# Sigmoid-weighted pooling on one core: goods loads issued at four places of an iteration, left-over weights laid out one copy at a time

## The chip, the cores and the metric

The kernel runs on one core of a Trainium2 chip. The metric is the device time in microseconds of one execution. Before the change the median of three runs is 299.17 us (297.19 to 300.1).

## The reference, cut to what matters

For each of B = 2048 rows there are N = 200 goods vectors of K = 32 numbers and one candidate vector of 32. The outer product of candidate and goods, the goods and the candidate go through a 1088 x 36 layer, a sigmoid and a 36 x 1 layer; the scalar weight that comes out weighs the goods, which are summed over N:

```python
outer = jnp.einsum('bi,bnj->bnij', candidate_ad, goods).reshape(Bs, Ns, Ks * Ks)
k_b = jnp.broadcast_to(candidate_ad[:, None, :], (Bs, Ns, Ks))
h1 = jnp.concatenate((k_b, goods, outer), axis=-1)
act = jax.nn.sigmoid(h1 @ W1 + b1)
weight = act @ W2 + b2
out = jnp.sum(goods * weight, axis=1)
```

All data are float32. goods is 52.4 MB and is read once.

## The kernel before

The outer product is never formed. In a setup stage the kernel folds each candidate into the first layer, so that each row has its own 32 x 36 weight (`wm` for the first 32 outputs, `wx` for the left-over 4). After that goods is streamed once.

Four rows are a unit, 8 units are a "pair" (two halves `s` of four units), and 64 pairs (`PAIRS`) are worked through in a software pipeline with `LAG` = 3. In iteration p of the main loop TensorE does, in this order:

1. `products(p)` (L267): 64 matmul records, goods times `wm`, into `z_ps` (or `s_ps`);
2. `spread(p - 3, 0)` (L332): spreads the weights of an older pair over partitions;
3. `row_sums(p - 1)` (L309): the second layer of the pair before, 24 records;
4. `products_x(p)` (L286): the left-over 4 outputs, 16 records;
5. `spread(p - 3, 1)` (L332).

ScalarE applies the sigmoids: eight `act` activations (L378; `act_done` counts up after each second one) and then one `actx` (L383, `actx_done`). VectorE takes the weights out of PSUM (`whole`, L408, `w_kept`) and pools pair p - 3 (L416; `pooled` counts up four times per pair, twice behind each `spread`). GpSimd splits the weights into three bf16 parts (L206, L208, L210, L215).

**Goods loads.** A pair is 800 KB, loaded by four DMAs of 200 KB, all issued by SyncE (SP) at L173. There are seven slots (`G_SLOTS`). The first seven pairs are loaded without a wait. From then on load j of pair p waits only for its own quarter of the slot: `pooled >= 4 * (p - 7) + j + 1`. So a load starts when VectorE has pooled that quarter of pair p - 7; `POOLED_ORDER` puts the quarters in the order in which they come free.

**Left-over weights.** `wx` is needed in a padded layout, which GpSimd writes in 8 chunks of 8 pairs. `lay_out(k)` (L189) makes the four copies of a chunk (L194). Two chunks are laid out before the loop; chunks 2 to 7 in the loop, all four copies in a row behind the split of every eighth pair. `products_x` waits at L277 for the chunk at each eighth pair.

**Instruction queue.** Each engine's program reaches it in 16 KB packets over the same DMA engines that carry goods; in the profile they are the packets of kind "instruction".

Of the kernel before, what the change touches and what calls it, by code (L numbers as in the profile page):

```python
# [13 lines left out]
HX = H - HM  # L14
UNITS = B // 4
PAIR_U = 8
PAIRS = UNITS // PAIR_U
G_SLOTS = 7
A_SLOTS = 3
LAG = 3  # L20
T_MAIN = HM // 4
# [2 lines left out]
WX_CHUNK = 8  # L24
# [18 lines left out]
def build(nc, goods_t, cand_r, cand_u, w1_outer, small, pick, out_t):  # L43
    with ExitStack() as ctx:
        def sb(name, shape, dt=F32):
            return ctx.enter_context(nc.sbuf_tensor(name, shape, dt))
# [4 lines left out]
        def sem(name):  # L51
            return ctx.enter_context(nc.semaphore(name))

        goods = sb("goods", [P, G_SLOTS, PAIR_U, N])
        wm = sb("wm", [P, UNITS // RUN, HM, RUN])
        wxd = sb("wxd", [P, UNITS // 2, 2, HX])
        warm = sb("warm", [P, 1])
        wx = sb("wx", [P, UNITS // 2, 3, 16])
        act = sb("act", [P, A_SLOTS, 4, 2 * N])
        actx = sb("actx", [P, A_SLOTS, N])  # L60
        consts = sb("consts", [P, C_ALL])
# [67 lines left out]
        pick_loaded = sem("pick_loaded")  # L129
        goods_loaded = [sem(f"goods_loaded{i}") for i in range(G_SLOTS)]  # L130
        out_stored = sem("out_stored")
        warm_set = sem("warm_set")
        wx_step = sem("wx_step")
# [4 lines left out]
        z_done = sem("z_done")  # L138
        x_done = sem("x_done")
        act_done = sem("act_done")  # L140
        actx_done = sem("actx_done")
# [8 lines left out]
        def kept(i, x):  # L150

            return 2 * i + x // 2 + 1
# [7 lines left out]
        @block.sync  # L160
        def _(sp):
            sp.dma_start(cand[:, :, :], cand_r[:, :, :]).then_inc(cand_loaded, 16)
            sp.dma_start(candu[:, :], cand_u[:, :]).then_inc(candu_loaded, 16)

            sp.wait_ge(w1_loaded, 16)
            sp.wait_ge(consts_loaded, 16)
            for p in range(PAIRS):
                for j, v in enumerate(POOLED_ORDER):
                    if p >= G_SLOTS:

                        sp.wait_ge(pooled, 4 * (p - G_SLOTS) + j + 1)
                    first = N * (PAIR_U * p + v)
                    sp.dma_start(goods[:, p % G_SLOTS, v:v + 2, :].rearrange("p u n -> p (u n)"),  # L173
                                 goods_t[:, first:first + 2 * N]).then_inc(goods_loaded[p % G_SLOTS], 16)
                q = p - G_SLOTS
                if q >= 0 and q % STORE == STORE - 1:
                    first = PAIR_U * (q + 1 - STORE)
                    sp.dma_start(out_t[:, first:first + PAIR_U * STORE],
                                 out_stage[:, first:first + PAIR_U * STORE]).then_inc(out_stored, 16)
            sp.wait_ge(pooled, 4 * PAIRS)  # L180
            first = PAIR_U * (PAIRS - STORE)
            sp.dma_start(out_t[:, first:], out_stage[:, first:]).then_inc(out_stored, 16)
            sp.wait_ge(out_stored, 16 * (PAIRS // STORE))

        @block.gpsimd
        def _(pool):
            nc.gpsimd.memset(wx[:, :, :, :], 0.0).then_inc(wx_step, 1)

            def lay_out(k):  # L189

                of = slice(4 * WX_CHUNK * k, 4 * WX_CHUNK * (k + 1))
                for r in range(4):
                    rows = slice(32 * r, 32 * r + 32)
                    nc.gpsimd.tensor_copy(wx[rows, of, 0::2, HX * r:HX * r + HX], wxd[rows, of, :, :]).then_inc(wx_step, 1)  # L194
                    pool.wait_ge(wx_step, 4 * k + r + 2)

            pool.wait_ge(wx_step, 1)

            pool.wait_ge(wb_kept[0], kept(0, 2))
            pool.wait_ge(wb_kept[1], kept(0, 3))  # L200
            for k in range(WX_AHEAD):
                lay_out(k)
            pool.wait_ge(consts_loaded, 16)
            for q in range(PAIRS):
                pool.wait_ge(w_kept, q + 1)
                nc.gpsimd.tensor_scalar(top[:, :], whole[:, q % 2, :], m1, None, ALU.mult).then_inc(part_step, 1)  # L206
                pool.wait_ge(part_step, 4 * q + 1)
                nc.gpsimd.tensor_tensor(rest[:, :], whole[:, q % 2, :], top[:, :], ALU.subtract).then_inc(part_step, 1)  # L208
                pool.wait_ge(part_step, 4 * q + 2)
                nc.gpsimd.tensor_scalar(mid[:, :], rest[:, :], m2, None, ALU.mult).then_inc(part_step, 1)  # L210
                pool.wait_ge(part_step, 4 * q + 3)
                if q >= 2:

                    pool.wait_ge(s_done, 2 * (q - 1))
                nc.gpsimd.tensor_tensor(stack[:, q % 2, :], rest[:, :], mid[:, :], ALU.subtract).then_inc(part_step, 1)  # L215
                k = q // WX_CHUNK + WX_AHEAD
                if q % WX_CHUNK == 0 and k < PAIRS // WX_CHUNK:
                    pool.wait_ge(part_step, 4 * q + 4)
                    lay_out(k)

        @block.tensor
        def _(pe):
# [68 lines left out]
            def row_sums(p, step):  # L291
# [10 lines left out]
                for t in range(4):  # L302

                    if step < 2:
                        first = N * (t // 2)
                        left, right = w2m[:, step, :], act[:, p % A_SLOTS, 2 * (t % 2) + step, first:first + N]
                    else:
                        left, right = w2x[:, t, :], actx[:, p % A_SLOTS, :]
                    last = nc.tensor.matmul(w_ps[32 * t:32 * t + 32, 0:N], left, right,  # L309
# [46 lines left out]
        def _(sc):  # L356
# [14 lines left out]
            for p in range(PAIRS):  # L371
                if p >= A_SLOTS:

                    sc.wait_ge(w_done, p - A_SLOTS + 1)
                for r in range(4):
# [119 lines left out]
```

## Time and profile before

| | us |
|---|---|
| median of three runs | 299.17 |
| the profiled execution's own time | 294.3 |
| its span | 292.5 |
| TensorE matmul busy | 266.1 (91%) |
| ScalarE busy | 206.5 (71%) |
| GpSimd busy | 195.9 (67%) |
| VectorE busy | 195.7 (67%) |
| goods queue, share of the 16 DMA engines | 61.3% |

Matmul records overlap and their ends are modelled, so a high share says which engine sets the pace and not that it is at its peak. TensorE's granted clock is full in all slices but the last.

### The profile page before, as it was taken

What the parts mean: (1) busy time and instruction counts of PE and PEld (TensorE: products, weight loads), DVE (VectorE), ACT (ScalarE), POOL (GpSimd) and SP (SyncE); (2) the same over time, 40 slices, a digit from 0 to 9 for tenths busy, and PEclk for the clock granted to TensorE, in tenths of its full rate; (3) what the DMA queues carried; (4) which work ended last, traced back from release to release, by engine and by line L of the source; (5) the groups of instructions that cost most, each with busy time, mean ns of one, the idle gap of its engine ahead of it and who ended that gap; (6) DMA issues with size and microseconds to landing.
All of it is one profiled execution on the core that took longest, in us unless ns stands there. A gap on an engine that the chain in (4) does not pass through costs nothing.

```text
span 292.5 us, 17763 instructions
## 1 busy us (share of the span) xinstructions
PE 266.1 (91%) x7480; PEld 162.8 (56%) x7480; DVE 195.7 (67%) x1109; ACT 206.5 (71%) x596; POOL 195.9 (67%) x293
## 2 busy tenths in 40 slices
PE   1997999979999999999899997999989999899942
PEld 0363666546666556666566664665656656456620
DVE  0584177657777667777677775776757767667766
ACT  2486987757888768788777876877777767768720
POOL 9900597558677876688567874787656666667770
PEclk9999999999999999999999999999999999999995
DMA  6894057757777767677676875777666867665000
GB/s 240 255 366 171 4 155 217 211 162 212 223 210 229 210 193 227 220 227 230 167 230 207 229 229 163 221 222 215 192 192 177 263 173 215 194 185 152 6 0 9
DMA packets 38238, 55.59 MB, mean 190 GB/s; under 512 B 4240, under 2 KB 37904, under 8 KB 38032
## 3 DMA queue, kind: packets, MB, share of 16 engines
q1 hardware_dynamic: 37728, 54.02, 61.3%
q8 instruction: 59, 0.97, 1.3%
q10 hardware_dynamic: 432, 0.45, 0.4%
q14 instruction: 19, 0.16, 0.2%
HBM read 54.19 MB, written 0.26 MB: 186 GB/s over the span
## 4 chain that ended last, share of the span: by engine, by line
PE 86%; issue 4%; DVE 4%; ACT 3%; DMA 2%; DVEq 0%
PE z_ps L267 28%; PE w_ps L309 26%; PE x_ps L286 16%; PE s_ps L332 6%; PE x_ps L332 6%; DVE goods L416 3%; ACT wm L369 2%; PE s_ps L267 2%; DMA act<-w_outer 2%; PE z_ps L234 1%; PE x_ps L234 1%; DVE wxd L395 1%; ACT act L378 1%; PE w_ps L234 0%; DVE bias L398 0%
## 5 line engine op out<-in xcount | busy, mean ns | idle before, releaser
L378 ACT ACTIVATE act<-z_ps,bias 128x200 f32<-128x200 f32 x448 | 150.4, 442 | 54.0 <-PE z_ps L267 52.7
L416 DVE CUSTOM_DVE_ANT_0 goods<-s_ps,goods 128x200 f32<-128x200 f32 x252 | 81.9, 363 | 38.4 <-PE w_ps L332 38.4
L206 POOL TENSOR_SCALAR top<-whole,consts 128x200 bf16<-128x200 f32 x64 | 50.1, 783 | 70.0 <-DVE whole L408 69.3
L267 PE MATMUL z_ps<-goods,wm 32*32 32x200 f32 x3584 | 90.4, 354 | 2.8 <-issue 2.6
L267 PEld LDWEIGHTS z_ps<-goods,wm 32*32 32x32 f32 x3584 | 58.3, 145 | 23.6 <-issue 16.9
L286 PE MATMUL x_ps<-goods,wx 128*32 128x200 f32 x1024 | 59.4, 334 | 3.7 <-issue 3.7
L416 DVE CUSTOM_DVE_ANT_0 goods<-x_ps,goods 128x200 f32<-128x200 f32 x128 | 41.8, 364 | 29.8 <-PE s_ps L332 29.5
L309 PE MATMUL w_ps<-act,consts 128*32 128x200 f32 x1024 | 58.2, 339 | 1.4 <-DVE out_stage L416 1.4
L210 POOL TENSOR_SCALAR mid<-rest,consts 128x200 bf16<-128x200 f32 x64 | 50.1, 783 | 6.3
L286 PEld LDWEIGHTS x_ps<-goods,wx 128*32 128x32 f32 x1024 | 36.0, 109 | 16.1 <-issue 7.7
L332 PE MATMUL s_ps<-stack,pick_sb 64*128 64x200 bf16 x252 | 43.6, 254 | 1.5 <-DVE out_stage L416 1.5
L416 DVE DVE_READ_ACCUMULATOR2_ANT out_stage<- 128x1 f32 x512 | 42.7, 83 | 0.0
L416 DVE CUSTOM_DVE_ANT_0 goods<-w_ps,goods 128x200 f32<-128x200 f32 x128 | 41.4, 361 | 0.0
L215 POOL TENSOR_TENSOR stack<-rest,mid 128x200 bf16<-128x200 f32 x64 | 36.4, 568 | 5.5 <-PE w_ps L332 0.2
L208 POOL TENSOR_TENSOR rest<-whole,top 128x200 f32<-128x200 f32 x64 | 36.3, 568 | 5.3
L267 PE MATMUL s_ps<-goods,wm 32*32 32x200 f32 x512 | 38.9, 355 | 0.8 <-issue 0.8
L309 PE MATMUL w_ps<-actx,consts 128*32 128x200 f32 x512 | 35.5, 333 | 3.2 <-issue 3.2
L309 PEld LDWEIGHTS w_ps<-act,consts 128*32 128x32 f32 x1024 | 27.5, 109 | 18.1 <-issue 13.2
L408 DVE TENSOR_SCALAR whole<-w_ps,consts 128x200 f32<-128x200 f32 x64 | 27.2, 426 | 15.2 <-PE w_ps L309 15.2
L383 ACT ACTIVATE actx<-x_ps,biasx 128x200 f32<-128x200 f32 x64 | 29.8, 465 | 8.6 <-PE x_ps L286 8.5
L332 PEld LDWEIGHTS s_ps<-stack,pick_sb 64*128 64x128 bf16 x252 | 14.0, 95 | 21.2 <-DVE whole L408 17.3
L378 ACT ACTIVATE act<-s_ps,bias 128x200 f32<-128x200 f32 x64 | 25.1, 469 | 0.0
(40 smaller groups left out, 189.2 us busy)
## 6 DMA issues: line engine op xcount, KB each, us to landing
goods<-goods_t SPq DMA_DIRECT2D x256, 200.0 KB, 3.1
act<-cand_r SPq DMA_DIRECT2D x1, 1024.0 KB, 5.3
act<-cand_u SPq DMA_DIRECT2D x1, 256.0 KB, 6.0
out_t<-out_stage SPq DMA_DIRECT2D x4, 64.0 KB, 3.1
consts<-small ACTq DMA_DIRECT2D x1, 164.5 KB, 6.2
act<-w_outer ACTq DMA_DIRECT2D x1, 144.0 KB, 5.5
pick_sb<-pick ACTq DMA_DIRECT2D x1, 128.0 KB, 5.9
```

The costliest lines, as they stand in the source:

```text
L206: nc.gpsimd.tensor_scalar(top[:, :], whole[:, q % 2, :], m1, None, ALU.mult).then_inc(part_step, 1)
L208: nc.gpsimd.tensor_tensor(rest[:, :], whole[:, q % 2, :], top[:, :], ALU.subtract).then_inc(part_step, 1)
L210: nc.gpsimd.tensor_scalar(mid[:, :], rest[:, :], m2, None, ALU.mult).then_inc(part_step, 1)
L215: nc.gpsimd.tensor_tensor(stack[:, q % 2, :], rest[:, :], mid[:, :], ALU.subtract).then_inc(part_step, 1)
L267: last = nc.tensor.matmul(z_bank(p, r)[32 * c:32 * c + 32, N * s:N * s + N], wm[32 * r:32 * r + 32, u // RUN, :, u % RUN], goods[32 * r:32 ...
L286: last = nc.tensor.matmul(x_ps[32 * c:32 * c + 32, 0:N], left, goods[:, p % G_SLOTS, 4 * s + c, :], start=s == 0, stop=s == 1)
L309: last = nc.tensor.matmul(w_ps[32 * t:32 * t + 32, 0:N], left, right, start=step == 0, stop=step == 2)
L332: last = nc.tensor.matmul(s_bank(q, f, s)[:, N * i:N * i + N], pick_sb[rows, 2 * f + i, :], stack[rows, q % 2, :], start=True, stop=True)
L378: last = nc.scalar.activation(act[:, p % A_SLOTS, r, N * s:N * s + N], z_bank(p, r)[:, N * s:N * s + N], ACT.Sigmoid, bias=bias[:, r, p, s ...
L383: nc.scalar.activation(actx[:, p % A_SLOTS, :], x_ps[:, 0:N], ACT.Sigmoid, bias=biasx[:, p:p + 1]).then_inc(actx_done, 1)
L408: nc.vector.tensor_scalar(whole[:, p % 2, :], w_ps[:, 0:N], b2, None, ALU.add).then_inc(w_kept, 1)
L416: last = nc.vector.tensor_tensor_reduce(goods[:, q % G_SLOTS, v, :], s_bank(q, f, s)[:, N * i:N * i + N], goods[:, q % G_SLOTS, v, :], 1.0 ...
```

## The change

It changes two things on two engines that do not compute the long chain: SyncE's waits before the goods loads, and the place of GpSimd's layout copies.

```diff
+AHEAD = 3
...
+            def in_iteration(i, j):
+
+                if j == 0:
+                    sp.wait_ge(actx_done, i)
+                if j == 1:
+                    sp.wait_ge(z_done, 4 * i + 1)
+                if j == 2:
+                    sp.wait_ge(act_done, 4 * i + 1)
+                if j == 3:
+                    sp.wait_ge(act_done, 4 * i + 3)
+
             for p in range(PAIRS):
                 for j, v in enumerate(POOLED_ORDER):
                     if p >= G_SLOTS:
 
                         sp.wait_ge(pooled, 4 * (p - G_SLOTS) + j + 1)
+                    if p > AHEAD:
+
+                        in_iteration(p - AHEAD, j)
...
-            def lay_out(k):
+            def lay_out(k, r):
 
                 of = slice(4 * WX_CHUNK * k, 4 * WX_CHUNK * (k + 1))
-                for r in range(4):
-                    rows = slice(32 * r, 32 * r + 32)
-                    nc.gpsimd.tensor_copy(wx[rows, of, 0::2, HX * r:HX * r + HX], wxd[rows, of, :, :]).then_inc(wx_step, 1)
-                    pool.wait_ge(wx_step, 4 * k + r + 2)
+                rows = slice(32 * r, 32 * r + 32)
+                nc.gpsimd.tensor_copy(wx[rows, of, 0::2, HX * r:HX * r + HX], wxd[rows, of, :, :]).then_inc(wx_step, 1)
+                pool.wait_ge(wx_step, 4 * k + r + 2)
...
             for k in range(WX_AHEAD):
-                lay_out(k)
+                for r in range(4):
+                    lay_out(k, r)
...
                 k = q // WX_CHUNK + WX_AHEAD
-                if q % WX_CHUNK == 0 and k < PAIRS // WX_CHUNK:
+                if q % 2 == 0 and k < PAIRS // WX_CHUNK:
+
                     pool.wait_ge(part_step, 4 * q + 4)
-                    lay_out(k)
+                    lay_out(k, q % WX_CHUNK // 2)
```

On SyncE, the first load and those behind it, before the change (`goods` is the buffer, `goods_t` the input; 27 loads follow the first without a wait, and then 64 wait for `pooled` alone until the first store of results):

```order
L173 DMA goods<-goods_t 128x400 [waits consts_loaded,w1_loaded]
L173 DMA goods<-goods_t 128x400 x27
L173 DMA goods<-goods_t 128x400 [waits pooled] x64
L178 DMA out_t<-out_stage 128x128
```

and with the change:

```order
L188 DMA goods<-goods_t 128x400 [waits consts_loaded,w1_loaded]
L188 DMA goods<-goods_t 128x400 x15
L188 DMA goods<-goods_t 128x400 [waits actx_done]
L188 DMA goods<-goods_t 128x400 [waits z_done]
L188 DMA goods<-goods_t 128x400 [waits act_done] x2
...
L188 DMA goods<-goods_t 128x400 [waits actx_done,pooled]
L188 DMA goods<-goods_t 128x400 [waits z_done,pooled]
L188 DMA goods<-goods_t 128x400 [waits act_done,pooled] x2
```

Sixteen loads instead of 28 go out at once; each further one also waits for a point of the iteration three before the one that uses it, set by ScalarE, TensorE, ScalarE and ScalarE.

On GpSimd, behind the split of the ninth pair, before (`wxd` is the packed source of `wx`):

```order
L215 TENSOR_TENSOR stack<-rest,mid 128x200 [waits s_done,part_step]
L194 COPY wx<-wxd 32x32x2x4 [waits part_step]
L194 COPY wx<-wxd 32x32x2x4 [waits wx_step] x3
L206 TENSOR_SCALAR top<-whole,consts 128x200 [waits w_kept,wx_step]
L208 TENSOR_TENSOR rest<-whole,top 128x200 [waits part_step]
```

and with the change:

```order
L208 COPY wx<-wxd 32x32x2x4 [waits part_step]
L221 TENSOR_SCALAR top<-whole,consts 128x200 [waits w_kept,wx_step]
L223 TENSOR_TENSOR rest<-whole,top 128x200 [waits part_step]
L225 TENSOR_SCALAR mid<-rest,consts 128x200 [waits part_step]
L230 TENSOR_TENSOR stack<-rest,mid 128x200 [waits s_done,part_step]
```

The same 24 copies of the loop stand there, one behind every second pair of the first 48 in place of four behind every eighth.

## Rows read from the trace of the kernel before

**Rows 1.** The page: busy time by engine, and the chain by engine
```profile
PE 266.1 (91%) x7480; PEld 162.8 (56%) x7480; DVE 195.7 (67%) x1109; ACT 206.5 (71%) x596; POOL 195.9 (67%) x293
...
PE 86%; issue 4%; DVE 4%; ACT 3%; DMA 2%; DVEq 0%
```
**Rows 2.** The chain in order of time, starts of row_sums: start us, us, what
```profile
40.21 1.15 PE w_ps L309 x24
...
120.53 1.15 PE w_ps L309 x24
...
139.02 1.15 PE w_ps L309 x24
...
277.27 1.15 PE w_ps L309 x24
```
**Rows 3.** Waits: engine, line, releaser: us in total, times, longest
```profile
PEld z_ps L267 <- issue: 16.9, 72, 2.5
PEld w_ps L309 <- issue: 16.4, 70, 1.9
```
**Rows 4.** Timeline of weight loads: start, us, idle before and its cause
```profile
177.50 0.53 PEld L286 LDWEIGHTS x_ps<-goods,wx 128*32 128x32 f32 x16 [2.14 <-issue]
...
203.30 0.19 PEld L267 LDWEIGHTS s_ps<-goods,wm 32*32 32x32 f32 x4 [0.60 <-issue]
```
**Rows 5.** Windows: length, then busy us (x instructions) of PE, PEld, DVE, ACT, POOL
```profile
171.18:177.42 6.24, 4.57 (x128) 2.92 (x125) 3.95 (x24) 4.71 (x15) 4.12 (x7) 1.00 0.75 226
198.79:203.29 4.50, 4.25 (x125) 2.58 (x126) 2.84 (x17) 3.33 (x10) 3.02 (x5) 1.00 0.68 201
79.66:83.38 3.72, 3.72 (x114) 2.46 (x112) 2.84 (x17) 2.75 (x9) 2.68 (x5) 1.00 0.71 218
272.35:276.35 4.00, 4.00 (x148) 2.62 (x129) 3.15 (x22) 3.03 (x10) 2.92 (x6) 1.00 0.01 4
```
**Rows 6.** DMA queues, 171 to 175 us: packets, MB, share of 16 engines
```profile
q1 hardware_dynamic: 588, 0.84, 70.0%
```
**Rows 7.** DMA queues, 175.06 to 175.20 us
```profile
q8 instruction: 1, 0.02, 42.2%
```
**Rows 8.** DMA queues, 200.6 to 200.7 us
```profile
q8 instruction: 1, 0.02, 71.7%
```
**Rows 9.** DMA queues, 277.15 to 277.25 us
```profile
q8 instruction: 1, 0.02, 80.9%
```
**Rows 10.** DMA queues, 81.25 to 81.35 us
```profile
q8 instruction: 1, 0.02, 59.9%
```
**Rows 11.** DMA busy tenths of the 40 slices from 79.66 to 83.35 us
```profile
DMA  4359999899995400060997935798998999541118
```
**Rows 12.** Timeline of SyncE in the iteration that begins at 79.66 us
```profile
80.46 0.33 SPq L173 DMA_DIRECT2D goods<-goods_t  x1
...
81.03 0.33 SPq L173 DMA_DIRECT2D goods<-goods_t  x1
...
82.08 1.02 SPq L173 DMA_DIRECT2D goods<-goods_t  x2
```
**Rows 13.** Timeline of ScalarE in the same iteration
```profile
79.52 0.44 ACT L383 ACTIVATE actx<-x_ps,biasx 128x200 f32<-128x200 f32 x1
80.92 2.67 ACT L378 ACTIVATE act<-z_ps,bias 128x200 f32<-128x200 f32 x8 [0.97 <-PE z_ps L267]
```
**Rows 14.** Timeline of GpSimd at a lay-out, 66 to 69 us
```profile
66.87 1.77 POOL L194 COPY wx<-wxd 32x256 f32<-32x256 f32 x4
68.73 0.78 POOL L206 TENSOR_SCALAR top<-whole,consts 128x200 bf16<-128x200 f32 x1
```
**Rows 15.** Timeline of GpSimd in an iteration without lay-out, 79.6 to 83.5 us
```profile
83.09 0.78 POOL L206 TENSOR_SCALAR top<-whole,consts 128x200 bf16<-128x200 f32 x1 [0.77 <-DVE whole L408]
```
**Rows 16.** The goods loads' line, from issue to landing
```profile
DMA to landing us min/median/max: 2.3/3.1/6.2
```
**Rows 17.** The page: instruction packets of the queue that serves TensorE's blocks
```profile
q8 instruction: 59, 0.97, 1.3%
```

## The prediction, made before the changed kernel ran

> **What bounds the kernel.** I read the page first. TensorE holds 86% of the chain and is 91% busy; no other engine passes 71% [rows 1]. So only what moves TensorE counts. Then I read the chain in order of time, at the starts of row_sums, which come once per iteration. From 120.53 to 139.02 are five iterations without a disturbance: 18.49 / 5 = 3.70 us each. From 40.21 (iteration 4) to 277.27 (iteration 63) are 59 iterations in 237.06 us, 4.02 us each [rows 2]. 59 x 3.70 = 218.2, so **18.9 us are lost** in the loop above TensorE's own pace, in single iterations that are 0.2 to 2 us too long.
>
> What causes them? The waits name no engine: the weight loads' largest sums are "issue", with longest waits of 2.5 and 1.9 us [rows 3]. Two such stalls in the timeline end at 177.50 (2.14 us idle) and 203.30 (0.60 us) [rows 4]. Between one stall's end at 198.79 and the next at 203.30 TensorE issued 125 matmuls and 126 weight loads, and before the stall at 177.50, from 171.18 on, 128 and 125 [rows 5]: with a few semaphore instructions some 256 each time, a fixed block, for each of which one 16 KB packet comes (59 packets, 0.97 MB [rows 17]). And a packet comes shortly before each stall ends. None is there from 171 to 175 [rows 6]; one starts at 175.07 and takes 0.42 x 16 x 0.14 = 0.95 us [rows 7], so TensorE goes on 1.5 us after its end. One starts at 200.64 and takes 0.717 x 16 x 0.1 = 1.15 us [rows 8]; TensorE goes on 1.5 us after it. So a stall is an **instruction packet that starts late**.
>
> How late may it be? An iteration has 112 weight loads, a block 125 [rows 5], so a block lasts 3.70 x 125 / 112 = 4.13 us. The packet seems to be asked for when a block begins. With the 1.0 us of the packet and the 1.5 us after it, it must start within 4.13 - 2.5, about 1.7 us, of that. Without goods traffic it does: the block from 272.35 ends at 276.35 (DMA share 0.01) [rows 5], and the next one's packet starts at 277.17 [rows 9], 0.8 us later. With traffic the waits are 1.85 us (198.79 to 200.64) and 3.9 us (171.18 to 175.07). So in the loop the pace is set by how long an instruction packet waits behind goods packets.
>
> **Part 1, the re-timed loads.** First how the packet waits. In the iteration from 79.66 the loads are issued at 80.46, 81.03, 82.08 and about 82.7 [rows 12]: two doublets 0.57 us apart, with 1.05 us from the second load to the third and about 1.5 us from the fourth to the next iteration's first. The DMA engines stand still in slices 14 to 16 (of 0.092 us each), from 80.95 to 81.24, are busy from about 81.4 to 82.9, and a few lag until 83.2 [rows 11]. So a doublet occupies the DMA 1.6 us, 0.8 us a load, from about 1.15 us after the first issue. The instruction packet of that time starts at 81.31 [rows 10], in the pause. I take this as the rule: **the packet starts in a pause between bursts**, once about 0.8 us of its own have passed, and may wait about 0.9 us beyond that before TensorE stalls.
>
> A pause opens where the next issue comes later than 1.6 - 0.57 = 1.03 us after the second of a doublet. Before the change the 1.5 us spacing always gives one, the 1.05 us spacing is on the edge. A burst of length b stalls a block by (b - 0.9)^2 / (2 x 3.70) us on average over where the block begins: doublets apart 2 x 0.07 = 0.13 us in both, merged (3.2 us) 0.71. The measured loss is 18.9 us over 59 x 112 / 125 = 53 blocks, 0.36 us each, so the edge pause opens in about 6 of 10.
>
> With the change, in times from the iteration's start (79.66): actx ends at 0.3 (79.52 + 0.44) to 0.6, the first half of `products` that counts `z_done` up at about 1.1 (0.15 us before the activations start), the second activation ends at about 2.0, the sixth at about 3.25 (eight in 2.67 us from 80.92) [rows 13]. Issues at 0.3 to 0.6, 1.1, 2.0, 3.25: spacings of 0.5 to 0.8, 0.9, 1.25, 0.7 to 1.0. The third load is on the edge (I say 1 in 2 that a pause opens ahead of it), ahead of the fourth a pause is sure (1.25 against 0.8), behind it likely (0.85, a single load needs 0.8). Bursts and their stalls: all pauses open 0.07; the first three loads merged (2.4 us) 0.30; the other merger 0.30; both 0.71. Weighted 0.43, 0.43, 0.07, 0.07 this is 0.03 + 0.13 + 0.02 + 0.05 = **0.23 us per block instead of 0.36**, or -36% of 18.9 us = **-6.8 us**. The ends: all pauses open gives 0.07, that is -15 us; the first three always merged and the fourth half of the time gives 0.5, that is +7 us.
>
> The page "DMA: Bandwidth & Descriptors" of the Trainium skill (section "Queues, rings and completion order") says that each DMA engine goes round its queues packet by packet, which would let an instruction packet in after one packet of goods. The trace disagrees: 588 goods packets passed from 171 to 175 while it waited; by that rule the re-timing would give 0.
>
> **More traffic early.** Before, 28 loads go out at once and the DMA is idle in the first iterations. Now 16 go out and loads run from iteration 1. Three to four more blocks meet traffic: at most 4 x 0.23 = +0.9, I take **+0.7 us**.
>
> **New waits on SyncE.** Behind each stand only later goods loads and four stores. Pair p's last load is issued 3.25 us into iteration p - 3, so 3 x 3.70 - 3.25 = 7.85 us ahead of its use; landing takes 3.1, at worst 6.2 us [rows 16]. `pooled` of pair p - 7 is then a whole iteration old. **0 us**; if the cover went, every iteration would pay for it. The one more wait per load is hidden by SyncE's idle time.
>
> **Part 2, the copies.** 24 copies of 0.44 us (1.77 / 4) move from six groups of four to 24 single places [rows 14]. Between two copies GpSimd waits 0.77 us for `whole` [rows 15], so one copy fits there in each second pair; before, a group pushed the next split back by 1.0 us (from idle 0.77 to a start at 68.73), which the two iterations until `spread` needs the split take in. The view of waits names nobody on TensorE that waited for a copy. The last copy of a chunk comes nine pairs before its use. **0 us**, and nothing to gain; upper bound of a gain, if each group had delayed TensorE by what exceeds the idle time, 6 x 1.0 = 6 us, for which no row speaks.
>
> **Sum.** -6.8 + 0.7 = -6.1 us. The profiled execution took 294.3 us, its sum is 288.2. The median of the runs is 4.9 us above the profiled one, so with the same difference: 299.2 - 6.1 = **293 us**.
>
> **Rivals.**
> *A, all pauses open.* Single loads end in less than 0.8 us, since the other engines need not wait for the slowest. For it: the mean share of 70%, 2.6 us of 3.7. Against it: the lagging engine in rows 11. Time 299.2 - 15 + 0.7 = 285.
> *B, spacing does not matter.* The same goods packets pass, and the wait depends on the share of busy time alone, or on one lagging DMA engine that is nearly full whatever the order. Time 299.2 + 0.7 = 300. "Instruction fetch mechanics" in the Trainium skill's page "Runtime: NRT & Kernel Launch" calls a block's fetch mostly hidden and gives TensorE room for 2048 instructions; were that so here, no stall of rows 4 would exist and nothing could be gained. The trace disagrees with the first half.
> *C, slower.* Three loads within 1.7 us run together (issues at 0.4, 1.1, 2.0), where before never more than two had to. A block whose packet is asked for in that burst waits up to 2.4 + 0.8 = 3.2 us and stalls 1.5 us; with the fourth merged half of the time 0.5 us per block, 53 x 0.5 = 26.5 against 18.9 us: +7.6 + 0.7, 307 us. It decides where a load holds the DMA longer than 0.9 us, the third's spacing. For it: the doublet's tail until 83.2.
> *D, the change does not do what it says*: `pooled` remains the later wait, and the loads stay where they are. Against it: `pooled` of pair p - 7 is done one iteration before. Under 1 in 20; I put it with B.
>
> **Chances.** Forecast 0.42 (three quarters of it more than 1% below), A 0.14, B with D 0.22, C 0.22. What this kernel's measurement can tell from no change is about 1%, 3 us. Faster by more than 1% (below 296.2): 0.31 + 0.14 = 0.45. Within: 0.11 + 0.19 = 0.30. Slower (above 302.2): C and a tenth of the others, 0.25. Range **284 to 305**: it takes in A and B, and the nearer half of C. The forecast's own range is 289 to 298.
>
> **What would show it.** In the profile of the changed kernel: the undisturbed pitch stays 3.70 us and the "issue" part of the chain falls from 4% to under 3%; the longest "issue" waits of the weight loads fall under 2 us; SyncE's issues stand at about 0.4, 1.1, 2.0 and 3.25 us of an iteration; DMA tenths show three pauses; GpSimd's copies stand alone, each beside a shorter wait for `whole`; the first iterations show DMA traffic. I am wrong if the pitch itself grows (then a load or `wx` is late), if TensorE waits for goods, or if stalls of 1.5 us and more become more frequent, each with an instruction packet that starts over 2 us into its block.

## The result: no faster

| | before | with the change |
|---|---|---|
| median, us | 296.69 (290.23 to 300.31, 20 runs) | 297.12 (293.97 to 301.74, 20 runs) |
| ratio, 95% interval | | 1.0129 (1.0081 to 1.0177) |
| the same pair measured once more | 299.79 | 298.77, ratio 1.0009 (0.9951 to 1.0068) |
| profiled execution | 294.3 | 301.74 |

Executions of one kernel scatter by 1.7% either way, and a ratio compares only those within 1.5% of their kernel's fastest, in the first comparison 6 of 20 before (the fastest, 290.23 us, sets the bar) and 15 of 20 with the change, so it need not be the quotient of the medians. The first ratio says 1.3% slower. Over all twenty the medians are 0.1% apart and the means 0.4% (297.34 against 296.13 us, interval -0.1 to +0.9%), and the second comparison says no difference. The forecast was 293.0 us, 2% faster than the 299.17 us known then. The time lies in the range, the gain is not there.

**The profile after.** Its page, busy time and the chain, as in [rows 1]:

```profile
PE 272.0 (91%) x7480; PEld 162.9 (54%) x7480; DVE 195.4 (65%) x1109; ACT 206.5 (69%) x596; POOL 196.3 (65%) x293
...
q1 hardware_dynamic: 37728, 54.02, 62.6%
...
PE 86%; issue 4%; DVE 4%; ACT 3%; DMA 2%; DVEq 0%
```

Nothing that computes changed, and the shares of the chain are those of before. The chain in order of time, starts of row_sums (start us, us, what), as in [rows 2]:

```profile
41.97 1.15 PE w_ps L325 x24
...
174.30 1.15 PE w_ps L325 x24
178.00 1.15 PE w_ps L325 x24
...
285.02 1.15 PE w_ps L325 x24
288.51 1.26 PE w_ps L325 x24
```

An undisturbed iteration still takes 3.70 us (174.30 to 178.00). Iterations 4 to 63 take 285.02 - 41.97 = 243.05 us, so by the prediction's own sum 243.05 - 218.2 = 24.9 us are lost, where [rows 2] gave 18.9. That is 6.0 of the 7.4 us between the two profiled executions. It can't be taken as the price of the change: the profiled execution with the change is the longest of its twenty, the one before is shorter than its median, and a second profile of the changed kernel (e5 below, 296.18 us) lost 21.6, one with the old places of the loads (e2) 25.1. Another 1.8 us lie ahead of iteration 4 (41.97 against 40.21), and the rest takes 0.4 us less. In windows (length, busy us of PE, PEld, DVE, ACT, POOL, then PEclk, DMA share, GB/s) the 1.8 us are the clock:

```profile
23.60:33.80 10.20, 9.87 (x216) 5.30 (x217) 0.65 (x2) 6.07 (x18) 1.05 (x2) 0.50 0.29 82
33.80:44.00 10.20, 10.20 (x322) 6.55 (x295) 4.87 (x27) 8.37 (x26) 8.09 (x14) 1.00 0.73 207
```

TensorE was granted 0.50, the 1.2 GHz level, for these 10 us, though it was busy in 9.87 of them. In the 5.6 us before them it had been busy for 4.31, in the profile of before for 5.60, where the clock stayed at 1.00. The second profile of the changed kernel (e5) shows 0.83 over the same 10 us and reaches row_sums of iteration 4 at 39.6, ahead of the 40.21 of before. So I do not put it down to the change. The waits of the weight loads (engine line, releaser: us in total, times, longest) show where in an iteration the 6.0 us lie:

```profile
PEld z_ps L283 <- issue: 22.1, 82, 2.5
...
PEld w_ps L325 <- issue: 16.8, 67, 1.7
PEld x_ps L348 <- issue: 9.8, 29, 1.6
```

Against [rows 3] `products` (z_ps) waits 5.2 us longer, row_sums (w_ps) 0.4. The longest wait, 2.5 us, stands ahead of the loop in both profiles. Inside the loop, stalls of 0.3 us and more at the border of an instruction block number 18 before and 31 with the change (29 in e5, and 27 in e2 below, which has the loads of before); stalls of 1.5 us and more fell from 2 to 1.

**The loads stand where they should.** SyncE in the iteration from 176.34 (start us, us, what; the second of two issues starts 0.33 us before the end):

```profile
176.01 1.28 SPq L188 DMA_DIRECT2D goods<-goods_t  x2
176.97 0.95 SPq L188 DMA_DIRECT2D goods<-goods_t  x2
178.43 0.33 SPq L188 DMA_DIRECT2D goods<-goods_t  x1
179.71 0.33 SPq L188 DMA_DIRECT2D goods<-goods_t  x1
```

The issues are at 176.97, 177.59, 178.43 and 179.71, that is 0.6, 1.25, 2.1 and 3.4 us into the iteration (forecast: 0.4, 1.1, 2.0, 3.25). What the DMA engines do in 176.34 to 180.04, busy tenths in 40 slices, as in [rows 11]:

```profile
DMA  9857766858896456767889385967968898848497
```

In [rows 11] four slices in the middle stand at 0 and three at the end at 1. Here one slice stands at 3 and all others at 4 or more: even spacing has not made more pauses, it has **taken the pauses away**. That holds for the loop: between iterations 4 and 56, stretches of 0.2 us and more with at most three goods packets under way number 48 before, 23 with the change and 25 in e5 (counted from the traces' packet records). The window says the same, DMA share 0.80 where [rows 5] has 0.71 (PEclk, DMA share, GB/s at the end):

```profile
176.34:180.04 3.70, 3.70 (x115) 2.37 (x113) 2.84 (x17) 2.98 (x10) 2.78 (x5) 1.00 0.80 224
```

And yet this iteration lost nothing. DMA queues (packets, MB, share of 16 engines), 170.40 to 171.20 us and then 171.20 to 172.10:

```profile
q1 hardware_dynamic: 158, 0.22, 97.2%
...
q1 hardware_dynamic: 124, 0.18, 66.7%
q8 instruction: 1, 0.02, 6.1%
```

In the 0.8 us ahead of this instruction packet the engines are 97.2% busy with goods, and the packet starts all the same and takes 0.061 x 16 x 0.9 = 0.88 us. No pause was needed. GpSimd's copies stand alone:

```profile
182.78 0.39 POOL L208 COPY wx<-wxd 32x256 f32<-32x256 f32 x1
183.51 0.78 POOL L221 TENSOR_SCALAR top<-whole,consts 128x200 bf16<-128x200 f32 x1 [0.34 <-DVE whole L424]
```

A copy of 0.39 us, and still 0.34 us of waiting for `whole` behind it (0.77 without a copy [rows 15]).

### The profile page after: what moved, and what is told of

It is laid out like the page before. It is cut to its first block, busy times and chain, and to the rows that moved or that the text cites. A ratio compares the mean times of both kernels' runs of the same rounds, so it can differ in the third digit from the quotient of the medians.

```text
span 299.9 us, 18009 instructions
## 1 busy us (share of the span) xinstructions
PE 272.0 (91%) x7480; PEld 162.9 (54%) x7480; DVE 195.4 (65%) x1109; ACT 206.5 (69%) x596; POOL 196.3 (65%) x293
## 3 DMA queue, kind: packets, MB, share of 16 engines
q1 hardware_dynamic: 37728, 54.02, 62.6%
## 4 chain that ended last, share of the span: by engine, by line
PE 86%; issue 4%; DVE 4%; ACT 3%; DMA 2%; DVEq 0%
PE z_ps L283 29%; PE w_ps L325 25%; PE x_ps L302 16%; PE s_ps L348 6%; PE x_ps L348 6%; ACT wm L385 3%; DVE goods L432 3%; PE s_ps L283 2%; DMA act<-w_outer 2%; PE z_ps L250 1%; DVE wxd L411 1%; PE x_ps L250 1%; DVE bias L414 0%; PE w_ps L348 0%; DVE out_stage L432 0%
## 5 line engine op out<-in xcount | busy, mean ns | idle before, releaser
L283 PE MATMUL z_ps<-goods,wm 32*32 32x200 f32 x3584 | 95.2, 361 | 3.7 <-issue 3.4
L283 PEld LDWEIGHTS z_ps<-goods,wm 32*32 32x32 f32 x3584 | 58.8, 145 | 28.7 <-issue 22.1
L302 PE MATMUL x_ps<-goods,wx 128*32 128x200 f32 x1024 | 60.3, 340 | 2.5 <-issue 1.5
L325 PE MATMUL w_ps<-act,consts 128*32 128x200 f32 x1024 | 58.1, 342 | 1.8 <-DVE out_stage L432 1.4
L283 PE MATMUL s_ps<-goods,wm 32*32 32x200 f32 x512 | 39.5, 360 | 1.5 <-issue 1.5
L348 PEld LDWEIGHTS s_ps<-stack,pick_sb 64*128 64x128 bf16 x252 | 14.1, 94 | 22.1 <-DVE whole L424 17.3
```

The source lines that it names most:

```text
L283: last = nc.tensor.matmul(z_bank(p, r)[32 * c:32 * c + 32, N * s:N * s + N], wm[32 * r:32 * r + 32, u // RUN, :, u % RUN], goods[32 * r:32 ...
L302: last = nc.tensor.matmul(x_ps[32 * c:32 * c + 32, 0:N], left, goods[:, p % G_SLOTS, 4 * s + c, :], start=s == 0, stop=s == 1)
L348: last = nc.tensor.matmul(s_bank(q, f, s)[:, N * i:N * i + N], pick_sb[rows, 2 * f + i, :], stack[rows, q % 2, :], start=True, stop=True)
```

## The experiments

Two numbers are read for each. "Lost" is the start of row_sums of iteration 63 less that of iteration 4, less 218.2 us, as above: 18.9 before, 24.9 with the change. "Wait" is the mean time from the beginning of a 256-instruction block on TensorE to the start of the next instruction packet, over the blocks of the loop, worked out from the trace's records: 1.93 us before, 2.10 with the change; where in its first instructions a block is taken to begin moves such a mean by some 0.05. Ratios are to the kernel before, measured in the same comparison.

### Each part alone

`e1_loads_only` has the re-timed loads and the copies of before, `e2_copies_only` the reverse.

```diff
--- e1_loads_only, against the changed kernel
-                if q % 2 == 0 and k < PAIRS // WX_CHUNK:
-                    lay_out(k, q % WX_CHUNK // 2)
+                if q % WX_CHUNK == 0 and k < PAIRS // WX_CHUNK:
+                    lay_out(k)          # all four copies
--- e2_copies_only, against the changed kernel
-                    if p > AHEAD:
-                        in_iteration(p - AHEAD, j)
```

> The kernel before with the re-timed goods loads alone; the copies of wx stay four in a row. Theory (the loads' new places make TensorE's instruction packets wait longer): the loop loses about 23 us above a pitch of 3.70 us as with the whole change, against 17 to 19 before, and the ratio to the kernel before is 1.010 to 1.020. Rival (the copies cost, or help): the ratio differs from that of the whole change, 1.013, by more than 0.01.

> The kernel before with the copies of wx alone moved, one behind every second pair; the loads as before. Theory: GpSimd's idle time of 0.8 to 1.0 us per pair takes a copy of 0.44 us, nobody waits for it, ratio 0.995 to 1.005. Rival (the copies are what made it slower): 1.01 or more.

Measured: e1 298.08 us, 0.9989 (0.9943 to 1.0036), lost 23.7, wait 2.09. e2 298.31 us, 0.9956 (0.9904 to 1.0008), lost 25.1, wait 2.10. Neither part does anything that can be measured; e1's expected 1.010 to 1.020 did not come. More is in e2: it has the loads of before, and its profile lost 25.1 us where the profile of before lost 18.9. So **the 6 us between the first two profiles is also the scatter between executions of one arrangement**, and the -36% of 18.9 us started from a favourable specimen (294.3 us; the medians of the kernel before in the five comparisons are 294.5 to 299.8).

### All four at one place, and the changed kernel again

`e3_one_place` takes the pauses' argument to its end: all four loads wait for `actx_done`. `e5_changed_again` is the changed kernel unaltered.

```diff
             def in_iteration(i, j):
-                if j == 0:
-                    sp.wait_ge(actx_done, i)
-                if j == 1:
-                    sp.wait_ge(z_done, 4 * i + 1)
...
+                sp.wait_ge(actx_done, i)
```

> The changed kernel, but all four loads of an iteration wait for actx_done alone, so they are issued back to back, once per iteration. The pause rule of my prediction (an instruction packet starts only in a pause between bursts): a burst holds the DMA 4 x 0.8 = 3.2 us of 3.7, 0.71 us lost per block, 38 us in all, about 315 us. Rival (one long pause per iteration serves as well as several short ones, and what counts is that there is a real pause at all): like before or better, 285 to 299 us.

> The changed kernel again, beside the kernel before on this chip, to see whether the ratio of 1.013 of the first comparison returns although each half alone gave 0.999 and 0.996. Theory (the places of the loads only shift which blocks of TensorE's program wait, the mean wait stays at 2.0 to 2.1 us): 0.995 to 1.01. Rival (the two halves together cost what neither costs alone): 1.01 to 1.02 again.

Measured: e3 300.56 us (290.15 to 305.62, no ratio; the kernel before 297.79), lost 28.0, wait 2.07. Merging four loads into one burst was to cost 15 us by the pause rule; it cost at most a few. e5 298.77 us, 1.0009 (0.9951 to 1.0068), lost 21.6, wait 2.01. The 1.3% did not come back.

### Loads placed by the blocks

Each block of 256 instructions begins at a fixed point of the program. `e4_clear` was to put the loads into the 2.5 us that begin 0.15 us behind a block's beginning, so that goods should be out of the way when the next packet is wanted; `e7_in_the_way` moves the same places by 1.75 us, to where they should hurt most.

```diff
+                part = (t - starts[k]) / (starts[k + 1] - starts[k])
+                return starts[k] + 0.15 + part * 2.5      # e7_in_the_way: 1.9 in place of 0.15
...
+                    at, s, c = max(late, key=lambda x: x[0])   # the last semaphore step before that time
+                    sp.wait_ge(s, c)
```

> The changed kernel with the loads' places set by TensorE's instruction blocks instead of by the iteration: the points of the program at which a block of 256 instructions begins are known from the trace (every 4.13 us, one iteration and 27 instructions apart), and each load waits for the last progress semaphore ahead of a place 0.15 to 2.65 us behind such a point, never in the 1.5 us before it. Theory (a packet is delayed by loads issued in the 1.3 us before its block begins): stalls of 0.3 us and more nearly vanish, the loop loses under 7 us, 280 to 288 us. Rival (it is the total traffic, or the time since the last block, and not where the loads stand): 295 to 300 us.

> The kernel of e4_clear with the places of the loads moved by 1.75 us against TensorE's blocks: 1.9 to 4.4 us behind a block's beginning, so just ahead of the next one. Theory of a harmful window (loads issued in the 1.3 us before a block begins delay its packet): slower than e4_clear, which avoided that window, 308 us and more. Rival (the window does not exist, and the fifth and sixth loads that both tables bunch together are what costs): the same as e4_clear or faster, 297 to 306 us.

Measured: e4 306.13 us, 1.0219 (1.0138 to 1.0300), lost 28.4, wait 2.14. e7 306.43 us, 1.0325 (1.0262 to 1.0388), lost 35.8, wait 2.22. But neither kernel does what its name says. Of e4's loads in the loop only half are issued 0.1 to 2.9 us behind a block's beginning, the median at 2.9, and 43% in the 1.3 us ahead of the next block, where none should be; in e7 that is 31%, as before the change (30%). The table of places counts on `pooled` at 0.8, 1.35, 2.35 and 2.95 us of an iteration, while the loads of the kernel before, which wait for it, go out at 2.39, 2.95 and, an iteration on, 0.80 and 1.37: 1.6 to 2.1 us later. So whether loads kept clear of the blocks would help was not tested.

What the two runs do show is the mean. Six kernels with four 200 KB loads (before, the changed one, e1, e2, e3, e4) have waits of 1.93 to 2.14 us whatever their places, and e7 is not far off. That was the forecast's rival B. Single blocks do depend on the place. Over 387 blocks of nine profiles with 200 KB loads (these seven, e5 and e13) the wait is 1.57 us on average where no load was issued in the 1.3 us before the block began, 2.01 with one, 2.16 with two and 2.56 with three. A block is 0.4 us longer than an iteration, so in a kernel whose loads stand at fixed places of an iteration the blocks drift past all of them, and the mean hardly moves.

### Without the traffic

`e6_no_loads` leaves the goods loads of pairs 7 to 63 out (it computes on old data, and `products` waits for a slot's first filling only), with the placement of before.

```diff
                     if p >= G_SLOTS:
+                        continue
```

> The kernel before without the goods loads of pairs 7 to 63 (the data of the slots are used again, so the values are others); nothing else is left out. In the changed kernels some instruction packets started 2.1 to 2.2 us into their block although no goods load was under way, all in blocks that begin 2.1 us into an iteration. Theory A (goods traffic alone makes packets late): all waits about 0.8 to 1.1 us, no stalls, the loop loses under 2 us, 276 to 279 us. Theory B (part of the wait belongs to where in TensorE's program the block begins): blocks that begin 1.3 to 2.8 us into an iteration wait 1.7 us and more with no traffic, the loop still loses 4 to 8 us, 280 to 287 us.

Measured: 280.85 us, 0.9476 (0.9425 to 0.9528), lost 7.2, wait 1.30. So of the 18.9 to 25 us, 12 to 18 are the price of goods traffic, and **7.2 us are lost without any**. What such a stall looks like: weight loads in the timeline, then DMA from 93.95 (a block begins) to 96.60, then the queue from 96.60 to 96.75.

```profile
97.81 0.30 PEld L310 LDWEIGHTS w_ps<-actx,consts 128*32 128x32 f32 x8
99.17 0.19 PEld L287 LDWEIGHTS x_ps<-goods,wx 128*32 128x32 f32 x8 [1.06 <-issue]
```

```profile
DMA  0000000000000000000000000500000000000000
...
q8 instruction: 1, 0.02, 42.0%
```

For 2.65 us the DMA carries one packet of another engine's program, then TensorE's packet starts (it takes 0.42 x 16 x 0.15 = 1.0 us), and TensorE goes on 1.5 us behind it. Nothing was in its way. Seven blocks of the loop wait like this, 2.3 to 2.8 us; by their place in the program they are seven of the nine that begin 1.6 to 2.2 us into an undisturbed iteration. The others wait 1.1 us on average (0.4 to 1.8). The same seven blocks can be followed through the other profiles. Their stalls add up to 6.3 us here, 8.2 before, 6.6 with the change and 4.9 in e10 below; those of all the other blocks to 1.0, 9.2, 16.6 (14.0 in e5, 17.4 in e2) and 4.0. So goods traffic takes its price almost wholly from blocks that would not stall without it. The waits by line:

```profile
PEld z_ps L268 <- issue: 14.0, 65, 2.5
PEld w_ps L310 <- issue: 13.3, 65, 1.6
```

`products` waits 14.0 us in all without traffic (most of it not stalls but short gaps, 65 of them), 16.9 before [rows 3], 22.1 with the change, but also 21.6 in e2 with the loads of before. This row is a ready gauge of what goods traffic cost in one profile.

### Larger loads

`e8_two_large_loads` loads a pair with two DMAs of 400 KB (3200 bytes per partition and row), each behind the pooling of its half (`pooled` 3 and 4), 0.8 and 1.4 us into an iteration. `e9_large_spread` lets the same two loads wait for `actx_done` and the first `act_done` as well. `e11_small_rows` goes the other way, 200 KB loads cut into rows of 800 bytes.

```diff
--- e8_two_large_loads, against before
-                for j, v in enumerate(POOLED_ORDER):
+                for j in range(2):
                     if p >= G_SLOTS:
-                        sp.wait_ge(pooled, 4 * (p - G_SLOTS) + j + 1)
+                        sp.wait_ge(pooled, 4 * (p - G_SLOTS) + j + 3)
...
+                                 goods_t[:, first:first + 4 * N]).then_inc(goods_loaded[p % G_SLOTS], 16)
--- e9_large_spread, against e8_two_large_loads
+                    if p > AHEAD and j == 0:
+                        sp.wait_ge(actx_done, p - AHEAD)
+                    if p > AHEAD and j == 1:
+                        sp.wait_ge(act_done, 4 * (p - AHEAD) + 1)
--- e11_small_rows, against before (the input padded, so that rows don't join)
-                                 goods_t[:, first:first + 2 * N]).then_inc(goods_loaded[p % G_SLOTS], 16)
+                                 goods_t[:, first:first + 2, 0:N]).then_inc(goods_loaded[p % G_SLOTS], 16)
```

> The kernel before with two loads of 400 KB per pair in place of four of 200 KB, each with rows of 3200 instead of 1600 bytes: the same bytes in half the packets. Load A waits for three quarters of its slot, load B for all. If what holds up an instruction packet is the number of goods packets ahead of it or their fixed cost: fewer stalls, 285 to 292 us. If it is the bytes, or how long the burst lasts: 297 to 303 us, since two loads 0.6 us apart are one burst of 800 KB.

> Two loads of 400 KB per pair as in e8_two_large_loads, at two of the changed kernel's places (actx_done of the iteration before, about 0.4 us into the iteration, and act_done of the first quarter, about 2.0 us) instead of together behind pooled. Theory (what counts is the number of rows that pass the DMA, not where the loads stand): like e8, 288 to 296 us, ratio 0.97 to 0.99. Rival (e8 gained from its one long pause per iteration, and spreading takes it away): 297 to 302 us.

> The kernel before, four loads of 200 KB per pair at the same places, but each with 256 rows of 800 bytes instead of 128 of 1600 (the input is padded between units so that rows do not merge). Row theory: twice the goods packets, instruction packets wait longer, 303 to 320 us. Rival (bytes alone count): ratio 0.995 to 1.01.

> e8_two_large_loads again, with more rounds, since its four runs lay between 288.8 and 306.3 us. If its gain of 2.3% is real: ratio 0.970 to 0.990. If it was drawn from few runs: 0.99 to 1.01.

Measured: e8 294.25 us, 0.9766 (0.9674 to 0.9859), lost 13.0, wait 1.64. The same kernel again as `e12_two_large_again` 288.9 us, 0.9748 (0.9631 to 0.9865), lost 9.4, wait 1.62. e9 302.15 us, 1.0267 (1.0170 to 1.0364), lost 26.0, wait 2.12. e11 301.51 us, 1.0143 (1.0033 to 1.0253), lost 21.9, wait 2.01. In e9 only the second load has moved. SyncE in an undisturbed iteration that begins at 134.43:

```profile
135.23 0.33 SPq L178 DMA_DIRECT2D goods<-goods_t  x1
136.52 0.33 SPq L178 DMA_DIRECT2D goods<-goods_t  x1
```

The first is issued at 0.80 us and not at 0.4, since `pooled` comes later than `actx_done`, and that is where e8 has it; the second is at 2.09 instead of 1.37. So the same two large loads gain 2.5% with the second at 1.37 and cost 2.7% with it 0.7 us later, and rival B is no general law either. That rows half as long cost something (e11) is not shown: two executions carry its ratio, and its loss of 21.9 lies between those of before and e2, which have the same places.

### One load: rows or place

`e10_one_load` loads a pair with one DMA of 800 KB (rows of 6400 bytes) as soon as the whole slot is pooled, 1.4 us into an iteration; `e15_one_load_again` repeats it. `e13_small_same_place` lets four 200 KB loads start at that same place, `e14_one_load_later` moves the one load 1.85 us later.

```diff
--- e10_one_load, against before
-                for j, v in enumerate(POOLED_ORDER):
-                    if p >= G_SLOTS:
-                        sp.wait_ge(pooled, 4 * (p - G_SLOTS) + j + 1)
+                if p >= G_SLOTS:
+                    sp.wait_ge(pooled, 4 * (p - G_SLOTS) + 4)
...
+                sp.dma_start(goods[:, p % G_SLOTS, :, :].rearrange("p u n -> p (u n)"),
+                             goods_t[:, first:first + PAIR_U * N]).then_inc(goods_loaded[p % G_SLOTS], 16)
--- e13_small_same_place, against before
-                        sp.wait_ge(pooled, 4 * (p - G_SLOTS) + j + 1)
+                        sp.wait_ge(pooled, 4 * (p - G_SLOTS) + 4)
--- e14_one_load_later, against e10_one_load
+                if p > 3:
+                    sp.wait_ge(act_done, 4 * (p - 3) + 3)
```

> The kernel before with one load of 800 KB per pair, rows of 6400 bytes, issued when the whole slot is free. Row theory: half the packets of e8 again, but each is longer; 284 to 292 us. Rival (burst theory: 800 KB in one piece hold up the instruction packet for the whole burst): 297 us and more.

> Four loads of 200 KB per pair, rows of 1600 bytes as in the changed kernel, but all four wait for the last quarter of the slot (pooled 4), so they go out one behind the other about 1.4 us into an iteration, where the single load of 800 KB went out that took 284.3 us. Theory 'place': what helps is one pause of 0.8 us in each iteration at the right place, however long the rows are; then this takes 284 to 289 us, the excess in the loop is under 11 us and the mean wait of an instruction packet under 1.7 us. Rival 'rows': what helps is that long rows are fewer packets that an instruction packet stands behind; then this takes 295 to 301 us as the loads at one place (actx_done) did, with a mean wait over 2.0 us.

> One load of 800 KB per pair, which besides its slot waits for act_done 4(p - 3) + 3, so it goes out about 3.25 us into an iteration instead of 1.4: the goods-free pause of some 0.8 us lies half an iteration later. Theory 'place': the pause must lie where instruction packets would start (0.5 to 2 us into an iteration); moved away it gives nothing, 293 to 303 us, and the mean wait of a packet is over 1.9 us. Rival 'rows': one load with rows of 6400 bytes helps wherever it stands; then 284 to 288 us with a mean wait under 1.7 us. Both hold each in part: 288 to 293 us.

> The kernel with one load of 800 KB per pair again, on another chip or at another time, as its 0.970 rests on four runs: 284 to 286 us and a ratio to the kernel before of 0.955 to 0.975. If the gain was luck of those runs, as the changed kernel's 1.013 did not come back in a second measurement, the ratio is 0.98 to 1.00.

| | us | ratio (interval) | lost | wait |
|---|---|---|---|---|
| e10_one_load | 284.3 | 0.9701 (0.9634 to 0.9767) | 9.2 | 1.55 |
| e15_one_load_again | 284.46 | 0.9712 (0.9644 to 0.9779) | 11.1 | 1.59 |
| e13_small_same_place | 298.11 | 1.0194 (1.0103 to 1.0285) | 23.1 | 2.00 |
| e14_one_load_later | 313.31 | 1.0688 (1.0602 to 1.0774) | 34.5 | 2.30 |

e13 came out as the rival "rows" had it, e14 slower than either theory allowed. Neither long rows nor the place is enough: **in the places tried the gain needs both**. Small loads started at the place give nothing, the large load 1.85 us later costs 6.9% by the ratio (5.7% by the medians, 313.31 against 296.28 us). One difference is left between e10 and e13: SyncE takes time for every issue, so the four small loads leave at 1.37, 1.75, 2.2 and 2.95 us (medians), the one large load all at 1.37. A burst of short rows as compact as e10's was not tried. Waits of e10 and then of e14:

```profile
PEld w_ps L307 <- issue: 15.2, 69, 1.6
PEld z_ps L265 <- issue: 13.6, 64, 2.5
```

```profile
PEld z_ps L267 <- issue: 29.8, 80, 2.5
PEld w_ps L309 <- issue: 14.5, 65, 1.6
```

In e10 `products` waits 13.6 us, as much as with no traffic at all (14.0); in e14 29.8. The DMA engines in one undisturbed iteration of each, 40 slices of 0.092 us: of e10 from 72.50, of e13 from 68.55.

```profile
DMA  9898993999949538000000000999529552991939
```

```profile
DMA  7928798943333210000000000554435999899898
```

e10 works until its 16th slice, 1.5 us into the iteration, and is then idle for nine slices, 0.83 us. e13's first load is issued at the same point and its engines are idle for ten slices, but the end of its burst is ragged: from the ninth slice on fewer than half of the engines still work. What that tail means for the instruction packet I can't show, since the records don't say which DMA engine carries it.

A pause is not the whole of it either. In e10, DMA queues from 56.40 to 57.00 and from 57.00 to 57.95:

```profile
q1 hardware_dynamic: 36, 0.23, 96.9%
...
q1 hardware_dynamic: 60, 0.38, 97.6%
q8 instruction: 1, 0.02, 5.8%
```

The packet starts in the midst of a full burst, on one of the 16 engines, while 15 carry goods. In e14 no packet comes in a stretch that is less full, 80.8%, and idle at its beginning (a store of results is among its transfers): DMA queues from 102.60 to 106.05 and from 106.05 to 107.05, and the weight loads behind it.

```profile
DMA  0009994691043143779599597897597795696352
...
q1 hardware_dynamic: 283, 0.88, 80.8%
...
q8 instruction: 1, 0.02, 5.8%
q1 hardware_dynamic: 6, 0.00, 0.7%
```

```profile
108.51 0.14 PEld L286 LDWEIGHTS x_ps<-goods,wx 128*32 128x32 f32 x3 [2.48 <-issue]
```

This block began at 101.71. No instruction packet for TensorE starts until the burst has ended, 4.37 us later, and TensorE stands still for 2.48 us. The same block waits 1.8 us in e6, without goods. The Trainium skill's page "DMA: Bandwidth & Descriptors" (section "Queues, rings and completion order") has each DMA engine change queues after a packet of goods. The rows of e10 fit that. Those of e14 don't, unless the packet was asked for only when the burst was nearly over, and when it is asked for no record shows.

## Why the prediction was wrong

**What held.** TensorE sets the pace, its undisturbed iteration is 3.70 us before and after. In every profile all stalls of 0.7 us and more in the loop end at the border of a 256-instruction block, 1.1 to 1.7 us behind the end of an instruction packet; the forecast had 1.5. SyncE's new waits cost 0: the loads stand at the forecast phases, land in 3.0 us at the median (2.3 to 5.6), and no wait of TensorE names them. The copies cost 0 and gain 0 (e2 0.9956, interval up to 1.0008). `pooled` is not a whole iteration old, as the prediction has it: the third and fourth quarters are pooled at 0.80 and 1.37 us of the iteration in which the loads for them go out at 2.1 and 3.4, which is early enough. The first iterations do carry more traffic, share 0.73 from 33.8 to 44.0; its +0.7 us can't be told from the clock beside it.

**The step that failed** is Part 1, the rule "the packet starts in a pause between bursts" and the -36% made from it. Three things speak against it.
1. Packets start in full traffic: the 97.2% above. Of 54 packets of the loop, 39 start while eight or more goods transfers are under way with the change, 28 before, where only 7 start with no goods transfer under way. The rule rested on one packet [rows 10] that stood in a pause.
2. The pauses didn't come. I reckoned a 200 KB load as a block of 0.8 us, so that a gap opens wherever the spacing is larger. The DMA tenths show no such block: a load alone is drawn out, and four of them evenly spaced fill the iteration. Nor is idle time what pays. With no goods packet under way on any engine, as a share of iterations 4 to 56: 4.3% before, 1.2% with the change, 17.7% in e10 and 27.5% in e14, the slowest of all.
3. The places tried for small loads don't matter for the mean wait: 1.93 to 2.14 us in six kernels, with the four loads in doublets (before), spread (e1) or together (e3). Measured per block, the change gives 24.9 / 53 = 0.47 us, and 21.6 / 53 = 0.41 in e5, against the forecast 0.23.

**Two more terms.** The loss that traffic could explain was too large from the start: 7.2 of the 18.9 us are there without goods (e6), from seven blocks above all that wait 2.3 to 2.8 us for a packet on an idle DMA. The prediction's longest wait, 3.9 us from 171.18, belongs to one of the seven: without goods the same block still waits 2.6 us (e6), so most of the time in which "588 goods packets passed" is not time behind goods. "The packet is asked for when a block begins, 0.8 us" was read from one block outside the loop. And the sum stood on one profile of 294.3 us whose loss of 18.9 is the smallest of the kernels with four 200 KB loads; the same loads lost 25.1 in e2.

**The rivals.** B (spacing doesn't matter, 300 us) comes nearest for small loads: 0.996 to 1.014 for the changed kernel, e1, e2 and e11, 1.019 to 1.033 for e13, e4 and e7. e8, e10 and e14 show that it isn't so for larger ones. C (slower, 307 us) had the sign of the first comparison and not the mechanism: e3 issued all four loads within 1.4 us, and its blocks wait 2.07 us, no longer than those of the changed kernel. A's condition, all pauses open, did not arise in the changed kernel.

**What stays open.** Why a block that begins 1.6 to 2.2 us into an iteration gets its packet so late with an idle DMA. Why a packet starts inside a full burst in e10 and only behind one in e14. What small loads would give that are really clear of the blocks. And whether the change costs nothing or a few tenths of a per cent: the two ratios, 1.013 and 1.001, have intervals that don't meet, but the first hangs on few executions of before, and all of them together give 1.004 (0.999 to 1.009). The same caution goes for the 1 to 2% of e11 and e13 (quotients of the medians 1.024 and 1.006), and not for 3% twice (e10, e15) or for e14.

## What to carry to other kernels

A stall whose releaser is only "issue" is worth a kernel without the data traffic before anyone re-times loads: it says in one run how much of the loss traffic explains at all, and here it left 12 of 19 us. It also shows which blocks stall anyway. Spreading transfers evenly filled the pauses here rather than making new ones; what paid was the opposite, one 800 KB load with long rows at one of the two points tried, 3% faster than the kernel before in two comparisons (0.9701 and 0.9712), and its place has to be measured, since 1.85 us later it costs 6.9%. An experiment on places needs a look at where the loads went, before its time is read: e4, e7 and e9 had them elsewhere than meant. A rule on waits should be checked on all the packets of the trace, not on the one that suggests it.

## What was not expected of the hardware

- TensorE can be short of instructions with idle DMA engines: 7.2 us of 281 in e6, single stalls of about 1 us.
- The number of packets mattered for the time that the same bytes occupy the DMA engines: the goods queue's 54.0 MB took 164 us in 10080 packets (e10), 179 in 37728 (before) and, in e11, 196 in 70496.

```profile
q1 hardware_dynamic: 10080, 54.01, 58.1%
```

- That row is e10's, 58.1% of a span of 282.4 us; before it is 61.3% of 292.5, in e11 65.9% of 297.1. From 179 to 164 us is 8% less. The Trainium skill ("DMA: Bandwidth & Descriptors", section "Bandwidth") advises batching DMAs to 1 MiB and more. Going from 200 to 800 KB agrees with it in occupied time; e14 shows that it decides nothing about the kernel's.
- The clock at the loop's beginning: 0.50 for 10.2 us in one profile of the changed kernel, 1.00 in that of before, 1.8 us of difference by iteration 4; another profile of the changed kernel (e5) has 0.83 over the same stretch, so executions of one kernel differ in it.
